# Two pre-norm decoder layers: norms on VectorE, value splits on GpSimd, 16-bit query products and a new order

## The chip, the cores and the metric

One core of a Trainium2 chip. TensorE multiplies, VectorE (DVE), ScalarE (ACT) and GpSimd (POOL) do the rest, SyncE (SP) issues most transfers. The metric is the device time of one execution in microseconds. The kernel before takes 503.5 us (median of three runs, 502.57 to 505.62).

## The reference

16 sequences of 128 tokens with 128 channels go through six residual layers. Each normalises its input first.

```python
def _layernorm(x, axis=-1, eps=1e-05):
    m = jnp.mean(x, axis=axis, keepdims=True)
    v = jnp.var(x, axis=axis, keepdims=True)
    return (x - m) / jnp.sqrt(v + eps)

x = x + _L0_attn_ref(_layernorm(x), ...)             # self0: 16 heads of 8, causal softmax
x = x + _L0_xattn_ref(_layernorm(x), ctx_1024, ...)  # cross0: 8 heads of 64 over 128 context rows
x = x + _L0_ffn_ref(_layernorm(x), ...)              # ffn: ternary weight, inputs rounded to 8 bits
x = x + _L1_attn_ref(_layernorm(x), ...)             # self1: scores clipped to +-10, causal
x = x + _L1_xattn_ref(_layernorm(x), ctx_1024, ...)  # cross1: 16 heads of 64
x = x + _L1_ffn_ref(_layernorm(x), ...)              # moe: softmax gate over 8 experts, gates under 0.1 dropped
```

In the cross layers q = x @ Wq, k = context @ Wk, v = context @ Wv, and the output is softmax(q k / scale) v @ Wo. All values are float32.

## The kernel before

**Stages and order.** Each sequence is one 128x128 tile. The six layers are stages named self0, cross0, ffn, self1, cross1, moe, and each is cut into steps such as `self0.rs` or `cross1.pv.0`. A planner (`all_steps`, `Plan`) knows of each step its engine, a cost, the steps that it needs and the PSUM banks that it takes; the order of the steps on each engine is written out by hand in `ORDER`, as strings of two letters per step, and each engine runs its list in that order with semaphore waits. Several sequences are under way at a time, and an engine that waits for one step holds all that stand behind it in its list. The banks of PSUM (8, single "X" ones for short fills, pairs "S" for scores) are handed out by the plan.

**A norm.** The residual step on VectorE ends with `stats` (line 1010): mean, and variance plus eps. Step `rs` on GpSimd (`rstd`, line 738) raises the variance to -0.5 (line 742), drains, and multiplies the mean by minus that (line 747). Step `nm` on ScalarE (`normalise`, line 887) then makes `xn` as Identity of x with a scale and a bias (line 893). Only sequence 0 of self0 does it on VectorE, with one `tensor_scalar` (line 1221). TensorE turns `xn` over (`xT`, line 1547), ScalarE copies it to `xnT` (`xTe`, helper `take`, line 830).

**A cross layer.** cross0 has one chunk of 8 heads, cross1 two. Step `q` (`four_pairs`, line 1288) multiplies four 128x128 blocks of the query weights with `xnT`, in float32 (line 1291), and ScalarE copies the result (`qe`). Keys and values of the context are made ahead: 6 sequences ahead for cross0, 4 for cross1 (`AHEAD`). Each is a sum of three products of high and low parts (lines 1392 to 1402). For the values, ScalarE writes the high part as bfloat16 into `v_high` (`ve`, line 948), and VectorE subtracts it from PSUM and writes the low part as float16 into `v_low` (`vl`, line 1051).

**The weights of attention.** `s1` makes the scores (line 1333), VectorE their negative maxima (`mx`, line 1045), ScalarE the exponentials e (`ex`, line 865) and their float16 high part (`hi`, line 874). SyncE turns that over by a transposing DMA (`dh`, line 697), GpSimd writes the low part beside it (`lo`, line 781), SyncE turns that over too (`dm`, line 703). `pv` multiplies both with the values, three products per head (lines 1373 to 1375), and VectorE divides by the sums (`nr`, lines 1061 and 1063). The next sequence's `ex` of a chunk waits until `lo` has read e; the next `lo` waits until `dm` has read the low part.

**Other work of GpSimd** that stands around the change: the low parts of the self layers' weights, in place (line 774), the split of their small values (lines 764 and 766), the low parts of large weights once at the start (line 643), the sum over the experts (lines 796 to 802).

Of the kernel before, what the change touches and what calls it, by code (L numbers as in the profile page):

```python
# [28 lines left out]

SHIFT = 7 * math.log(2.0)  # L30
# [53 lines left out]
def all_steps():  # L84
# [9 lines left out]
    def norm(L, source, users, read="xTe"):  # L94
        add(f"{L}.rs", "POOL", 940, [source], [f"{L}.nm"], first=580 if L == "self0" else None,
            last=580 if L == "moe" else None)
        add(f"{L}.nm", "ACT", 380, [but_last(f"{L}.rs") if L == "moe" else f"{L}.rs", source],
            [f"{L}.un" if L == "ffn" else f"{L}.xT"], first=300 if L == "self0" else None, last=170 if L == "moe" else None)
# [3 lines left out]
        made = dict(ffn=["ffn.un"], moe=[but_last("moe.nm"), last_only(source)]).get(L, [f"{L}.nm"])  # L102
        fill(f"{L}.xT", 109, made, f"{L}.{read}", users)
        add(f"{L}.xTe", *(("DVE", 250) if L == "ffn" else ("ACT", 332 if L == "moe" else 166)),
            [f"{L}.xT", *([last_only("moe.nm")] if L == "moe" else [])])

    def self_attention(L, source, maxima, following, loads, loads_out):
# [24 lines left out]
        add(f"{L}.res", "DVE", 835, [f"{L}.y"], [f"{following}.rs"])  # L132

    def keys_values(L, chunks, k_w, v_w):
# [4 lines left out]
        for c in range(chunks):  # L139
            fill(f"{L}.v.{c}", 695, [*context, f"{v_w}.lo"], f"{L}.vl.{c}", [ago(f"{L}.pv.{c}", AHEAD[L])])  # L140
            add(f"{L}.ve.{c}", "ACT", 484, [f"{L}.v.{c}"])
            add(f"{L}.vl.{c}", "DVE", 605, [f"{L}.ve.{c}"])

    def cross_attention(L, source, chunks, following, biased, k_w, v_w, loads):
        keys_values(L, chunks, k_w, v_w)
        norm(L, source, [f"{L}.q.{c}" for c in range(chunks)])
        for c in range(chunks):
            fill(f"{L}.q.{c}", 893, [f"{L}.xTe", loads], f"{L}.qe.{c}", [f"{L}.s1.{c}"])
            add(f"{L}.qe.{c}", "ACT", 487, [f"{L}.q.{c}"])
        for c in range(chunks):  # L150
            add(f"{L}.s1.{c}", "PE", 893, [f"{L}.qe.{c}", second(f"{L}.ke.{c}")], (), "S", f"{L}.ex.{c}")
            add(f"{L}.mx.{c}", "DVE", 1130, [f"{L}.s1.{c}"], [f"{L}.ex.{c}"])
            add(f"{L}.ex.{c}", "ACT", 2060, [f"{L}.mx.{c}"], [f"{L}.lo.{c}"], half=1030)
            add(f"{L}.hi.{c}", "ACT", 940, [f"{L}.ex.{c}"], [f"{L}.dh.{c}"])
            add(f"{L}.dh.{c}", "SP", TURN, [f"{L}.hi.{c}"], [f"{L}.T.{c}"], tail=TURN_TAIL)
            add(f"{L}.lo.{c}", "POOL", 2100, [f"{L}.hi.{c}"], [f"{L}.dm.{c}"])
# [5 lines left out]
        fill(f"{L}.y", 893, [f"{L}.oTe.0"], f"{L}.res", last=1116 if chunks == 2 else None)  # L162
        if chunks == 2:
            add(f"{L}.z", "PE", 893, [f"{L}.y", f"{L}.oTe.1"])
        add(f"{L}.res", "DVE", 840, [f"{L}.{'yz'[chunks - 1]}", *biased], [f"{following}.rs"],
# [304 lines left out]
def decoder(nc, t, out):  # L470
    ctx = ExitStack()
    with ctx:
# [249 lines left out]
        def _(pool):  # L722
# [15 lines left out]
            def rstd(L, i):  # L738
# [876 lines left out]
```

## Time and profile before

| what | value |
|---|---|
| runs | 503.5 us median, 502.57 to 505.62 |
| the profiled execution | 504.29 us, of which the span is 502.5 us |
| granted TensorE clock, mean over the span | 0.983 |
| TensorE busy | 471.4 us, 94% |
| ScalarE busy | 438.6 us, 87% |
| VectorE busy | 404.4 us, 80% |
| GpSimd busy | 383.4 us, 76% |

A line of the page names a group of instructions: source line, engine, operation, tiles, shapes, count, then busy time and mean duration in ns, then the idle time in front of them and what ended it. PE is TensorE, PEld its weight loads, DVE VectorE, ACT ScalarE, POOL GpSimd, SP SyncE. A busy share of the whole span mixes a start, a middle and a tail.

### The profile page before, as it was taken

The page shows a single profiled execution, that of the slowest core. Times are in us where ns is not written, and L with a number is a line of the kernel's source. Part 1 is how long each engine was busy: PE and PEld are TensorE (multiplying, and loading weights), DVE is VectorE, ACT ScalarE, POOL GpSimd, SP SyncE. Part 2 cuts the span into 40 slices and gives each one's busy share as a digit, 9 for nine tenths or more (in the row PEclk, how much of TensorE's full clock was granted, in tenths as well). Part 3 has the DMA queues.
Part 4 walks back from the last instruction along what each step waited for, and adds up shares of the span by engine and source line. Part 5 has one row for each costly group of instructions (what it writes and reads, how often), then busy time and mean ns, then how long its engine had stood idle before and what let it go on. Part 6 is the DMA issues. An engine that isn't in the chain of part 4 may idle for free.

```text
span 502.5 us, 16468 instructions
## 1 busy us (share of the span) xinstructions
PE 471.4 (94%) x5702; PEld 399.1 (79%) x5702; DVE 404.4 (80%) x954; ACT 438.6 (87%) x1180; POOL 383.4 (76%) x465
## 2 busy tenths in 40 slices
PE   7789998999999999999999999999999899999866
PEld 3678786787888898877888888897788788978764
DVE  4598887986888888888889898888987678867645
ACT  4688889999999989998989999999889898999842
POOL 2487587877668878889979888996877599775752
PEclk8799999998999999999999999999999999999989
DMA  6800222205132422531254215243424224233450
GB/s 195 330 3 3 43 43 44 43 10 115 24 68 45 85 44 42 94 65 39 48 92 87 55 29 79 44 90 46 85 53 84 57 44 86 43 65 71 89 97 16
DMA packets 107841, 33.87 MB, mean 67 GB/s; under 512 B 102768, under 2 KB 106224, under 8 KB 107760
## 3 DMA queue, kind: packets, MB, share of 16 engines
q1 hardware_dynamic: 107328, 32.04, 31.8%
q8 instruction: 47, 0.77, 0.6%
q10 hardware_dynamic: 432, 0.79, 0.5%
q14 instruction: 34, 0.28, 0.2%
HBM read 6.50 MB, written 1.05 MB: 15 GB/s over the span
## 4 chain that ended last, share of the span: by engine, by line
PE 59%; ACT 10%; POOL 9%; issue 9%; DMA 3%; POOLq 3%; DVE 3%; SPq 2%; DVEq 1%; ACTq 0%
PE psum L1291 6%; PE psum L1333 5%; PE psum L1419 5%; PE psum L1342 4%; POOL w_self L774 4%; PE psum L1322 4%; POOL e_parts_cross L781 3%; PE psum L1382 3%; ACT w_cross L865 3%; DMA eT_cross<-e_parts_cross 2%; PE psum L1431 2%; PE psum L1392 2%; PE psum L1373 2%; PE psum L1400 2%; PE psum L1355 2%
## 5 line engine op out<-in xcount | busy, mean ns | idle before, releaser
L774 POOL TENSOR_TENSOR w_self<-w_self 128x1024 f16<-128x1024 f32 x64 | 120.9, 1900 | 19.8 <-ACT w_self L854 14.3
L781 POOL TENSOR_TENSOR e_parts_cross<-w_cross,e_parts_cross 128x1024 f16<-128x1024 f32 x48 | 102.6, 2141 | 13.0 <-ACT e_parts_cross L874 13.0
L865 ACT ACTIVATE w_cross<-psum,row_max_cross 128x128 f32<-128x128 f32 x384 | 105.0, 413 | 3.7 <-DVE row_max_cross L1045 3.4
L1045 DVE TENSOR_REDUCE row_max_cross<-psum 128x8 f32<-128x1024 f32 x48 | 58.3, 1219 | 7.9 <-PE psum L1333 7.5
L1333 PE MATMUL psum<-kT_cross,qT_cross 64*128 64x128 f32 x768 | 54.7, 284 | 0.6 <-ACT qT_cross L830 0.6
L1333 PEld LDWEIGHTS psum<-kT_cross,qT_cross 64*128 64x128 f32 x768 | 46.4, 187 | 8.4 <-issue 5.2
L874 ACT ACTIVATE e_parts_cross<-w_cross 128x1024 f16<-128x1024 f32 x48 | 52.6, 1099 | 0.3
L1373 PE MATMUL psum<-v_high_cross,eT_cross 128*128 128x65 bf16 x384 | 40.6, 196 | 5.5 <-DMA eT_cross<-e_parts_cross 3.7
L1373 PEld LDWEIGHTS psum<-v_high_cross,eT_cross 128*128 128x128 f16 x384 | 35.7, 98 | 10.5 <-issue 8.9
L1083 DVE SCALAR_TENSOR_TENSOR w_self<-psum,s_bound 128x1024 f32<-128x1024 f32 x32 | 37.9, 1219 | 4.3 <-PE psum L1322 3.6
L1072 DVE TENSOR_REDUCE row_max_self<-psum 128x8 f32<-128x1024 f32 x32 | 38.9, 1216 | 2.9 <-PE psum L1322 2.8
L1074 DVE TENSOR_TENSOR w_self<-psum,row_max_self 128x1024 f32<-128x1024 f32 x32 | 39.2, 1225 | 2.4
L1374 PE MATMUL psum<-v_low_cross,eT_cross 128*128 128x64 f16 x384 | 40.5, 193 | 0.0
L1375 PE MATMUL psum<-v_high_cross,eT_cross 128*128 128x65 bf16 x384 | 40.4, 194 | 0.0
L1322 PE MATMUL psum<-by_head_self,plain_self 32*128 32x512 f32 x256 | 37.4, 654 | 1.3 <-ACT by_head_self L830 1.1
L848 ACT ACTIVATE w_self<-w_self,shift 128x1024 f32<-128x1024 f32 x32 | 37.1, 1172 | 1.4 <-DVE w_self L1083 1.4
L854 ACT ACTIVATE w_self<-psum 128x1024 f32<-128x1024 f32 x32 | 33.3, 1040 | 5.2 <-PE psum L1342 4.9
L830 ACT ACTIVATE by_head_self<-psum,head_mask 128x128 f32<-128x128 f32 x128 | 37.4, 407 | 0.0
L1051 DVE TENSOR_TENSOR v_low_cross<-psum,v_high_cross 128x512 f16<-128x512 f32 x48 | 32.2, 676 | 6.2 <-ACT v_high_cross L948 5.9
L1063 DVE TENSOR_TENSOR eT_cross<-psum,e_rec_cross 128x512 f32<-128x512 f32 x48 | 33.2, 692 | 3.6
L1374 PEld LDWEIGHTS psum<-v_low_cross,eT_cross 128*128 128x128 f16 x384 | 35.8, 100 | 0.2
L1375 PEld LDWEIGHTS psum<-v_high_cross,eT_cross 128*128 128x128 f16 x384 | 35.9, 97 | 0.0
(221 smaller groups left out, 1539.9 us busy)
## 6 DMA issues: line engine op xcount, KB each, us to landing
eT_cross<-e_parts_cross SPq DMA_TRANSPOSE x96, 3.1
out_dram<-x_all SPq DMA_DIRECT2D x16, 64.0 KB, 2.0
x_all<-in_x SPq DMA_DIRECT2D x1, 768.0 KB, 7.8
cT_all<-in_ctx SPq DMA_DIRECT2D x1, 768.0 KB, 9.6
e_k<-in_e_k SPq DMA_DIRECT2D x1, 512.0 KB, 5.5
e_v<-in_e_v SPq DMA_DIRECT2D x1, 512.0 KB, 6.4
e_q<-in_e_q SPq DMA_DIRECT2D x1, 512.0 KB, 8.6
e_o<-in_e_o SPq DMA_DIRECT2D x1, 512.0 KB, 9.6
```

The lines of the kernel that those rows point to most:

```text
L774: pool.tensor_tensor(L.w_low[u], L.w[u][:], halves(L.w[u][:]), ALU.subtract)\
L781: pool.tensor_tensor(L.e_parts[u][:, UN:2 * UN], L.e[u][:], L.e_parts[u][:, 0:UN], ALU.subtract)\
L865: last = act.activation(L.e[u][:, P * p:P * (p + 1)], S_[:, P * p:P * (p + 1)], ACT.Exp, bias=L.row_max[:, u, p:p + 1])
L874: act.activation(L.e_parts[u][:, 0:UN], L.e[u][:], ACT.Copy).then_inc(L.e_high[u], 1)
L1045: dve.tensor_reduce(L.row_max[:, u, :], group(i, turn)[:].rearrange("p (h k) -> p h k", h=UNIT), AX_X, ALU.max, negate=True).then_inc(L.ma ...
L1072: dve.tensor_reduce(L.row_max[:, u, :], scores, AX_X, ALU.max)
L1074: dve.tensor_tensor(L.diff[u][:].rearrange("p (h k) -> p h k", h=UNIT), scores, L.row_max[:, u, :].unsqueeze(2).broadcast_to([P, UNIT, P]) ...
L1322: last = pe.matmul(group(i, name, u)[:, 512 * half:512 * (half + 1)], L.plain[rows, :], L.by_head[rows, :, :].rearrange("p j n -> p (j n)" ...
L1333: last = pe.matmul(S_[:, at:at + P], L.qT[rows, h // 2, :], kT[rows, h // 2, i % 2, :], start=True, stop=True)
L1373: pe.matmul(out_[:, at:at + XD + 1], e_high, v_high[:, UNIT * c + h, :], start=True, stop=False)
L1374: pe.matmul(out_[:, at:at + XD], e_high, v_low[:, UNIT * c + h, :], start=False, stop=False)
L1375: last = pe.matmul(out_[:, at:at + XD + 1], e_low, v_high[:, UNIT * c + h, :], start=False, stop=True)
```

## The change

Parts of the diff follow, each behind a sentence on it.

The norms of self0, cross0, ffn, self1 and cross1 move from ScalarE to VectorE, as one operation on x, the mean (a scalar per row) and the reciprocal deviation (one column, spread over 128). GpSimd no longer makes the negative mean for them. The norm of moe stays.

```diff
                 power = pool.tensor_tensor(L.rstd[:], L.mean_var[:, 1:2], minus_half[:], ALU.pow)
-                if (L, i) in ((self0, 0), (moe, NSEQ - 1)):
+                if L is not moe or i == NSEQ - 1:
                     power.then_inc(L.rstd_ready, 1)
                     return
                 pool.drain()
...
+            def normalise(L, i):
+                dve.wait_ge(L.rstd_ready, i + 1)
+                if i and L is not ffn:
+                    dve.wait_ge(x_full, full(i - 1, f"{L.name}.xT"))
+                if i and L is ffn:
+                    dve.wait_ge(units_ready, i)
+                dve.scalar_tensor_tensor(out=L.xn[:], in0=x_all[:, i, :], scalar=L.mean_var[:, 0:1],
+                                         in1=L.rstd[:].broadcast_to([P, P]), op0=ALU.subtract, op1=ALU.mult)\
+                    .then_inc(L.xn_ready, 1)
```

The values are written as float32 into one buffer `v`; their high part is the upper half of each word, read as bfloat16, and GpSimd puts the low part as float16 into the lower half. `pv` waits for that (`v_split`).

```diff
-        self.v_high = [self.sb(f"v_high{b}", [P, heads, XD + 1], BF16) for b in range(AHEAD[name])]
-        self.v_low = [self.sb(f"v_low{b}", [P, heads, XD], FP16) for b in range(AHEAD[name])]
+        self.v = [self.sb(f"v{b}", [P, heads, XD + 1]) for b in range(AHEAD[name])]
+        self.v_high = [by_halves(v, BF16)[:, :, :, 1] for v in self.v]
+        self.v_low = [by_halves(v, FP16)[:, :, 0:XD, 0] for v in self.v]
...
+def by_halves(v, dt):
+
+    return v[:].rearrange("p h w -> p (h w)").bitcast(dt).rearrange("p (h w two) -> p h w two", w=XD + 1, two=2)
...
+            def low_values(L, i, u):
+                buffer, heads = i % AHEAD[L.name], slice(UNIT * u, UNIT * (u + 1))
+                pool.wait_ge(*emptied(i, f"{L.name}.v.{u}"))
+                pool.tensor_tensor(L.v_low[buffer][:, heads, :], L.v[buffer][:, heads, 0:XD],
+                                   L.v_high[buffer][:, heads, 0:XD], ALU.subtract).then_inc(L.v_split[u], 1)
```

The low part of the attention weights goes into the first half of the buffer of e itself. So the next exponentials of a chunk wait for the transposition of the low part, and GpSimd waits for nothing there.

```diff
-        self.e_parts = [self.sb(f"e_parts{u}", [P, 2 * UN], FP16) for u in range(self.units)]
+        self.high_plane = [self.sb(f"high_plane{u}", [P, UN], FP16) for u in range(self.units)]
+        self.low_plane = [w[:].bitcast(FP16)[:, 0:UN] for w in self.w]
...
                 pool.wait_ge(L.e_high[u], i + 1)
-                if i:
-                    pool.wait_ge(L.e_turned[u], 16 * i)
-                pool.tensor_tensor(L.e_parts[u][:, UN:2 * UN], L.e[u][:], L.e_parts[u][:, 0:UN], ALU.subtract)\
+                pool.tensor_tensor(L.low_plane[u], L.e[u][:], L.high_plane[u][:], ALU.subtract)\
                     .then_inc(L.e_low[u], 1)
...
                 act.wait_ge(L.max_ready[u], i + 1)
                 if i:
-                    act.wait_ge(L.e_low[u], i)
+                    act.wait_ge(L.e_turned[u], 16 * i)
```

The queries become three float16 products. The weights, times 4096, are split once into high (ScalarE) and low (VectorE). ScalarE writes `xnT` as float16, VectorE its low part from PSUM in a new step `xl`, and `q` waits for that. The copy behind it divides by 4096.

```diff
+            def low_queries(name):
+                dve.wait_ge(hi_ready[name], 1)
+                dve.scalar_tensor_tensor(out=q_low[name], in0=wt[name][:], scalar=Q_UNIT, in1=q_high[name][:],
+                                         op0=ALU.mult, op1=ALU.subtract).then_inc(lo_ready[name], 1)
+
+            def low_x(L, i):
+                name = f"{L.name}.xT"
+                dve.wait_ge(L.xnT_ready, i + 1)
+                dve.tensor_tensor(L.xnT_low[:], bank(i, name)[:, 0:P], L.xnT[:], ALU.subtract)\
+                    .then_inc(emptied(i, name)[0], 1)
...
                 for k in range(4):
-                    col = P * (4 * c + k)
-                    last = pe.matmul(bank(i, name)[:, P * k:P * (k + 1)], w[:, col:col + P], xT,
-                                     start=True, stop=True)
+                    col, out_ = P * (4 * c + k), bank(i, name)[:, P * k:P * (k + 1)]
+                    pe.matmul(out_, w_low[:, col:col + P], L.xnT[:], start=True, stop=False)
+                    pe.matmul(out_, w_high[:, col:col + P], L.xnT_low[:], start=False, stop=False)
+                    last = pe.matmul(out_, w_high[:, col:col + P], L.xnT[:], start=False, stop=True)
                 last.then_inc(x_full, 1)
```

In the planner the steps get new costs and needs, the loads a chain, and the `ORDER` strings of all five engines are new. On GpSimd, `m_w.lo` (2.4 us) moves from before the third pair of self0's low parts to behind the first ones of cross1, and the first value splits stand between the low parts of the start. On SyncE the transposes come in another order.

## Rows read from the trace of the kernel before

**Rows 1.** The page's first part: busy us, share of the span, instructions.
```profile
PE 471.4 (94%) x5702; PEld 399.1 (79%) x5702; DVE 404.4 (80%) x954; ACT 438.6 (87%) x1180; POOL 383.4 (76%) x465
```

**Rows 2.** Busy time by stretch: stretch, length, engines in the header's order, clock, DMA.
```profile
core 0: us, PE busy (x) PEld busy (x) DVE busy (x) ACT busy (x) POOL busy (x), PEclk, DMA share, GB/s
...
20.00:50.00 30.00, 28.42 (x283) 23.93 (x283) 24.33 (x37) 23.47 (x50) 21.34 (x30) 0.97 0.13 51
50.00:150.00 100.00, 94.21 (x1177) 78.94 (x1176) 81.78 (x177) 93.29 (x248) 74.45 (x89) 0.98 0.26 49
150.00:350.00 200.00, 198.08 (x2576) 171.66 (x2576) 174.77 (x412) 188.29 (x525) 171.94 (x206) 1.00 0.34 62
350.00:450.00 100.00, 95.94 (x1175) 82.16 (x1173) 81.31 (x197) 90.93 (x246) 79.52 (x95) 1.00 0.33 62
```

**Rows 3.** The chain that ended last, by engine, from the page.
```profile
PE 59%; ACT 10%; POOL 9%; issue 9%; DMA 3%; POOLq 3%; DVE 3%; SPq 2%; DVEq 1%; ACTq 0%
```

**Rows 4.** VectorE's waits, 150 to 350 us: total, times, longest (first, last).
```profile
DVE row_max_cross L1045 <- PE psum L1333: 2.0, 4, 0.6
...
DVE x_all L1112 <- PE psum L1492: 0.2, 1, 0.2
```

**Rows 5.** The same, 50 to 150 us (first and last).
```profile
DVE a_max L1019 <- ACT xn_ffn L893: 2.5, 2, 1.5
...
DVE e_rec_cross L1061 <- PE psum L1375: 0.2, 1, 0.2
```

**Rows 6.** The chain in order of time, 130 to 136 us: start, us, work.
```profile
130.08 0.03 PE psum L1373
...
131.34 0.12 PE psum L1393
...
133.63 0.89 PE psum L1291 x8
```

**Rows 7.** ScalarE's groups of instructions, 150 to 350 us.
```profile
L830 ACT ACTIVATE qT_cross<-psum 128x512 f32<-128x512 f32 x22 | 13.9, 634 | 0.5 <-PE psum L1291 0.5
L948 ACT ACTIVATE v_high_cross<-psum 128x512 bf16<-128x512 f32 x15 | 9.8, 653 | 0.1
L893 ACT ACTIVATE xn_cross<-x_all,minus_mean_cross,rstd_cross 128x128 f32<-128x128 f32 x14 | 7.3, 523 | 0.8 <-POOL minus_mean_cross L747 0.8
L893 ACT ACTIVATE xn_self<-x_all,minus_mean_self,rstd_self 128x128 f32<-128x128 f32 x14 | 7.3, 519 | 0.0
...
L893 ACT ACTIVATE xn_ffn<-x_all,minus_mean_ffn,rstd_ffn 128x128 f32<-128x128 f32 x7 | 3.6, 509 | 0.0
```

**Rows 8.** VectorE and GpSimd in order of time, 23 to 32 us: start, us, work.
```profile
23.61 3.75 POOL L774 TENSOR_TENSOR w_self<-w_self 128x1024 f16<-128x1024 f32 x2 [3.59 <-ACT w_self L854]
...
25.66 1.78 DVE L1197 TENSOR_SCALAR weighted<-weighted 128x128 f32<-128x128 f32 x1
...
27.32 2.37 POOL L643 TENSOR_TENSOR e_v_lo<-e_v,e_v_hi 128x1024 fp32r<-128x1024 f32 x1
27.52 2.25 DVE L1199 TENSOR_SCALAR ternary<-weighted 128x128 bf16<-128x128 f32 x1
...
31.30 0.29 DVE L1101 TENSOR_TENSOR attn_self<-o_sum_self,psum 128x128 f32<-128x128 f32 x1
...
31.50 0.68 DVE L1051 TENSOR_TENSOR v_low_cross<-psum,v_high_cross 128x512 f16<-128x512 f32 x1
```

**Rows 9.** GpSimd's groups of instructions, 150 to 350 us.
```profile
L774 POOL TENSOR_TENSOR w_self<-w_self 128x1024 f16<-128x1024 f32 x30 | 56.7, 1900 | 2.5 <-ACT w_self L848 1.9 <-ACT w_self L854 0.4
L781 POOL TENSOR_TENSOR e_parts_cross<-w_cross,e_parts_cross 128x1024 f16<-128x1024 f32 x22 | 47.0, 2143 | 5.2 <-ACT e_parts_cross L874 5.2
...
L764 POOL TENSOR_TENSOR v_self<-v_self 128x128 f32<-128x128 f32 x15 | 6.0, 402 | 0.0
```

**Rows 10.** The statistics' line 1013: duration in ns, least, median, most.
```profile
L1013 DVE BATCH_NORM_STATS2 moments_cross<-x_all x32: 294/295/297, 39.5 to 465.2; 128x6 f32<-128x128 f32 x32
```

**Rows 11.** The one norm on VectorE, line 1221: duration likewise.
```profile
L1221 DVE TENSOR_SCALAR xn_self<-x_all,mean_var_self,rstd_self x1: 347/347/347, 5.7 to 5.7; 128x128 f32<-128x128 f32 x1
```

**Rows 12.** DMA issues of the page: times issued, median us to landing.
```profile
eT_cross<-e_parts_cross SPq DMA_TRANSPOSE x96, 3.1
```

More of the change, by code:

```diff
@@ L28 @@
 CLIP = 10.0
+Q_UNIT = 4096.0
 SHIFT = 7 * math.log(2.0)
@@ L94, in norm @@
     def norm(L, source, users, read="xTe"):
[L95 to L98, printed above, removed]
+        if L == "moe":
+            add(f"{L}.rs", "POOL", 940, [source], [f"{L}.nm"], last=580)
+            add(f"{L}.nm", "ACT", 380, [but_last(f"{L}.rs"), source], [f"{L}.xT"], last=170)
+        else:
+            add(f"{L}.rs", "POOL", 580, [source], [f"{L}.nm"])
+            add(f"{L}.nm", "DVE", 200, [f"{L}.rs"], [f"{L}.un" if L == "ffn" else f"{L}.xT"])
         if L == "ffn":
@@ L139, in keys_values, with cross_attention @@
         for c in range(chunks):
[L140 to L144, printed above, removed]
+            fill(f"{L}.v.{c}", 695, [*context, f"{v_w}.lo"], f"{L}.ve.{c}", [ago(f"{L}.pv.{c}", AHEAD[L])])
+            add(f"{L}.ve.{c}", "ACT", 486, [f"{L}.v.{c}"])
+            add(f"{L}.vl.{c}", "POOL", 1000, [f"{L}.ve.{c}"])
+    def cross_attention(L, source, chunks, following, biased, q_w, k_w, v_w):
         keys_values(L, chunks, k_w, v_w)
@@ L161, in cross_attention @@
             add(f"{L}.oTe.{c}", "ACT", 486, [f"{L}.T.{c}"], [f"{L}.{'yz'[c]}"])
-        fill(f"{L}.y", 893, [f"{L}.oTe.0"], f"{L}.res", last=1116 if chunks == 2 else None)
+        fill(f"{L}.y", 893, [f"{L}.oTe.0", "in.more" if L == "cross0" else "in.cross1"], f"{L}.res", last=1116 if chunks == 2 else None)
         if chunks == 2:
             add(f"{L}.z", "PE", 893, [f"{L}.y", f"{L}.oTe.1"])
-        add(f"{L}.res", "DVE", 840, [f"{L}.{'yz'[chunks - 1]}", *biased], [f"{following}.rs"],
+        add(f"{L}.res", "DVE", 840, [f"{L}.{'yz'[chunks - 1]}", *biased], [f"{following}.{'rs' if following == 'moe' else 'nm'}"],
             last=780 if chunks == 2 else None)
-    for name, cost in (("x0", 3535), ("c0", 785), ("b_k", 1080), ("first", 600), ("b_v", 400), ("x1", 600),
-                       ("masks", 1800), ("more", 3600), ("e_k", 1400), ("e_v", 1400), ("x", 2000), ("ctx", 2200), ("self1", 600), ("cross1", 2500), ("moe", 1500)):
-        add(f"in.{name}", "SP", cost, once=True)
+    loads = (("x0", 3600), ("c0", 750), ("b_k", 1150), ("first", 500), ("b_v", 500), ("x1", 500), ("masks", 1500),
+             ("more", 4200), ("e_k", 1450), ("e_v", 1350), ("x", 2000), ("ctx", 2550), ("self1", 800),
+             ("cross1", 2600), ("moe", 1500))
+    for k, (name, cost) in enumerate(loads):
+        add(f"in.{name}", "SP", cost, [f"in.{loads[k - 1][0]}"] if k else [], once=True)
     add("consts", "POOL", 2700, once=True)
@@ L444, in __init__ @@
         self.e_turned = [self.sem(f"e_turned{u}") for u in range(self.units)]
-        self.v_made = [self.sem(f"v_made{u}") for u in range(self.units)]
+        self.v_split = [self.sem(f"v_split{u}") for u in range(self.units)]
 def halves(ap):
@@ L1413, in cross_project @@
                     room(i, y)
+                if i == 0 and c == 0:
+                    load = "more" if L is cross0 else "cross1"
+                    pe.wait_ge(loaded[load], load_count(load))
                 with_x = L is cross1 and i == NSEQ - 1
```

195 lines of the change are left out of this document (102 added, 93 removed).

## The prediction

> **What bounds the kernel now.** I read the busy shares of the page first [rows 1]: TensorE 94%, ScalarE 87%, VectorE 80%, GpSimd 76%. That is a mean over a start, a middle and a tail, so the busy time by stretch comes next [rows 2]. From 150 to 350 us TensorE is busy 198.1 of 200 us at a granted clock of 1.00 (its upper level, 2.4 GHz); ScalarE 188.3, VectorE 174.8 and GpSimd 171.9 stand close behind. The chain that ended last agrees: 59% TensorE, 10% ScalarE, 9% GpSimd, only 3% VectorE [rows 3]. So TensorE sets the pace of the middle, and the reader is to ask of each other engine how much more it can take.
>
> VectorE can take less than its share says. It is idle for 25.2 us of the middle, but its waits for another engine are 16 rows with a sum of 10.3 us, from 2.0 down to 0.2 [rows 4]. The other 14.9 us are short pauses behind its own dependent operations, which stay. So its spare time is 10.3 us of 200. From 50 to 150 us it is 11.4 us in 10 rows [rows 5].
>
> **Queries as 16-bit products.** A chunk of queries now takes 8 TensorE pieces of one chain entry, 0.89 us [rows 6]. After the change it is 12 products of 128 columns. No row has that size; two lie near. A key piece of 256 columns starts 0.12 us after the one before, 0.06 per 128 columns; a values product of 65 columns 0.03 us, 0.06 for 128 [rows 6]. Both carry a weight load of 128 columns each. I take 12 x 0.06 = 0.71 us, 0.18 us less per chunk; 48 chunks give 8.6 us of TensorE. The ends: 0.03 us each, if columns did not count, would save 25 us; 0.12 each would cost 26. Both rows scale with columns, so neither end is likely. VectorE gets 32 low parts of x, 14 of them in the middle (one per normalised x of a cross layer [rows 7]).
>
> **Low parts of the values.** VectorE loses 48 operations, 15 in the middle [rows 7]. One lasts 0.68 us, of which the next operation overlaps some 0.09, as it does with the one in front (31.30 + 0.29 against 31.50 [rows 8]): 0.60 us, 9.0 back in the middle. GpSimd gets them. Its in-place operation takes 0.40 us on 128 elements and 1.90 on 1024 [rows 9], so 1.04 on 512 by a straight line; the ends are half of 1.90 and half of 2.14 with a start of 0.1 on top. That is 15.6 us in the middle against what goes from there (next part). The values in TensorE's products are now every second 16-bit word. The key pieces already stream 4 bytes per column at 0.12 us for 256 columns, the same 0.47 ns per column as the values product [rows 6], so I price the stride at nothing; at half rate it would be 24 x 0.03 = 0.7 us per chunk.
>
> **In-place weights.** ScalarE's next exponentials wait for the transposition of the low part rather than for the subtraction, some microseconds more, once per sequence and chunk. What hides it is the period of a chunk, about 28 us (200 us hold seven FFN norms [rows 7]); GpSimd in turn no longer waits there. Price 0; without that cover, up to 3.1 us [rows 12] for each of 48. The transposes are as many and as large as before; SP's queue only issues them in another order. The split of the two query weights is ScalarE and VectorE work of some 1 us each, once, before the first queries.
>
> **The norms.** GpSimd drops the drain and the negative mean, and ScalarE loses 79 norms of 0.51 us, 40 us of busy time; in the middle 35 (14 + 14 + 7 [rows 7]), 18 us. ScalarE has cover from then on. GpSimd loses about 35 x (0.27 + 0.17) = 15.4 us of operation and pause there, which is what the values bring: no change.
>
> VectorE gets the norms. An operation of 128 elements occupies it for 0.20 us (31.30 to 31.50 [rows 8]): 7.0 us for 35. With 14 low parts of x at the same 0.20 (2.8) and the values gone (9.0), VectorE has 0.8 more in the middle. That would fit ten times over. What decides is whether a norm also waits. The old norm subtracted the mean on ScalarE; the new one reads x and the reciprocal deviation from SBUF as two tensors and writes SBUF, while GpSimd is busy 86% of the middle.
>
> No steady VectorE operation of the kernel before has that form: each has at least one tensor in PSUM, or one input only. The rows bound it. From below: the statistics read x from SBUF and write 6 numbers, and take 294 to 297 ns, whatever GpSimd does [rows 10]: no wait. From above, the nearest shape, 128x128 from SBUF to SBUF: two scalings of the ternary weights took 1.78 and 2.25 us, where the norm of sequence 0, with GpSimd idle, took 0.35 [rows 11]. The first began in GpSimd's pair of operations from 23.61 to 27.36 and ended at 27.44; the second began in the operation from 27.32 to 29.69 and ended at 29.77 [rows 8]. Each waited for the GpSimd operation that was running and went through 0.08 us after it.
>
> I take the upper row, since the norm is nearest to it: same size, nothing in PSUM. The price per norm is then the rest of the running GpSimd operation. For an arrival at any moment that is the sum of n x d x d / 2 over 200 us: 30 x 1.90 x 1.90 = 108 and 22 x 2.14 x 2.14 = 101 [rows 9], some 45 from the short ones: 254 / 400 = 0.63 us. I take 0.6. If each norm met a GpSimd operation at its very start, it would be 171.9 / 206 = 0.83 us [rows 2].
>
> The Trainium skill has a rule for this, in "SBUF — State Buffer", section "Who interferes with whom": a VectorE instruction with two SBUF inputs contends with a GpSimd instruction that reads SBUF, and the one that issues second blocks until the first ends. By that rule each norm waits and the time is the 515 us of the sum below; by the statistics' row it would be 494. The trace agrees for the one-input scalings (1.78 and 2.25 us); no run here shows the two-input form.
>
> **The sum**, against the profiled execution's 504.3 us (span 502.5 and 1.8 around it; 0.8 above the 503.5 median):
> - 150 to 350 us: VectorE gets 0.8 + 35 x 0.6 = 21.8 and has 10.3 free: +11.5. TensorE's saving of 22 chunks is worth nothing there, because VectorE is late: the norm is queued ahead of the maxima and quotients on its in-order engine, ScalarE's exponentials wait for the maxima, and TensorE for the banks that both empty.
> - 50 to 150 us: some 22 norms x 0.6 = 13.2 against 11.4: +1.8.
> - 350 to 450 us: some 16 norms, 9.6, fit in 18.7 idle [rows 2]; TensorE keeps 11 x 0.18: -2.0.
> - The rest, 5 chunks: -0.9.
>
> 504.3 + 11.5 + 1.8 - 2.0 - 0.9 = 514.7. **I forecast 515 us.** With 0.45 per norm it is about 508; with 0.83 the three stretches give +27, 530.
>
> **Rivals.**
> *No wait (faster).* The two-input form behaves as the statistics do. Then VectorE's load stays, TensorE gives 8.6, and ScalarE, busy 93.3 of 100 at 50 to 150 us [rows 2], frees about 2 of the 5.8 us that TensorE idles there: 504.3 - 10.6 = 494 (489 to 498). For it: no row shows the two-input form waiting. Against it: the scalings. It decides below 10 / 35 = 0.28 us per norm.
> *Half hidden.* The new order puts norms where GpSimd pauses or VectorE would wait anyway, 0.3 us each: 35 x 0.3 + 0.8 - 10.3 = +1.0 in the middle, the other 26 chunks give 4.7: 501 (498 to 506). Against it: GpSimd pauses only 28 of 200 us.
> *GpSimd becomes the bound at the start.* From 20 to 50 us it is busy 21.3 of 30 [rows 2]; ten value splits at 1.04 fill that. Without norm waits some 5 us of the 10 gained go: 499. Against it: the values are made several sequences ahead.
>
> **Chances.** Norm waits 0.53 (own range 506 to 524); no wait 0.28; half hidden 0.14; GpSimd 0.05. Range 491 to 524: it leaves out the lower third of "no wait" and the highest waits, under 0.2. About 1%, 5 us, can be told from no change. Faster by over 1% is most of "no wait": 0.27. Within 1%: most of "half hidden" and GpSimd, and the edges: 0.22. Slower by over 1%: 0.51.
>
> **What would show it.** Norm operations on VectorE with a mean near 0.9 us and a maximum near 2.2, each ending just after a GpSimd operation, and VectorE over 90% busy in the middle with TensorE waiting for it: the forecast. Norms at 0.25 to 0.35 us throughout: "no wait". Query groups should stand 0.71 us long in the chain, value splits near 1.04 us on GpSimd, GpSimd's weights at 2.14. The forecast fails if the wait per norm is under 0.28 us, or if the new order leaves VectorE more room than 10 us.

## The result and the profile after

The changed kernel takes 533.1 us (median of 4 runs, 532.1 to 535.0) against 503.8 us of the kernel before in the same session: a ratio of 1.058 (95% interval 1.053 to 1.063). The forecast was 515 us with a range of 491 to 524. The direction was right, and so was the wait of the norms; what that wait costs was not, and the time lies outside the range. Where some executions of a kernel came in a slower state, only the others count here and below.

The page of the changed kernel (its profiled execution took 532.15 us), the busy time by stretch with the columns of [rows 2], and the chain that ended last:

```profile
span 530.1 us, 16680 instructions
...
PE 469.9 (89%) x5894; PEld 393.9 (74%) x5894; DVE 442.9 (84%) x1019; ACT 413.7 (78%) x1103; POOL 414.7 (78%) x434
```

```profile
50.00:150.00 100.00, 88.17 (x1149) 73.41 (x1150) 86.31 (x183) 81.22 (x217) 76.77 (x76) 0.97 0.28 49
150.00:350.00 200.00, 180.60 (x2381) 153.37 (x2378) 178.12 (x405) 160.64 (x438) 162.03 (x170) 0.98 0.33 54
350.00:450.00 100.00, 93.62 (x1210) 79.08 (x1209) 87.83 (x211) 83.25 (x225) 84.85 (x86) 1.00 0.40 67
```

```profile
PE 41%; DVE 23%; DVEq 11%; issue 10%; ACT 6%; POOL 5%; DMA 2%; POOLq 0%; SPq 0%; ACTq 0%
```

VectorE's busy time grew by 38.5 us over [rows 1], and TensorE and ScalarE work less of each of these stretches than in [rows 2]. In the chain VectorE stands at 23% plus 11% of its sequencer, where [rows 3] has 3% and 1%. Where the time went can be read from TensorE's instructions: a pass now has 5894 instead of 5702. At the old pace 150 to 350 us would hold 2576 x 5894 / 5702 = 2663 of them; it holds 2381, so this stretch fell behind by 200 x (1 - 2381 / 2663) = 21 us. From 50 to 150 us it is 5.6 us, from 350 to 450 us 0.4. Together that is 27.2 of the 27.6 us by which the span grew. (This takes instructions as a measure of work, so it is an estimate.)

The norms of the changed kernel, with the least, median and longest duration in ns, and who waited for them:

```profile
L1054 DVE SCALAR_TENSOR_TENSOR xn_self<-x_all,mean_var_self,rstd_self x32: 310/392/2521, 6.0 to 467.5; 128x128 f32<-128x128 f32 x32
L1054 DVE SCALAR_TENSOR_TENSOR xn_cross<-x_all,mean_var_cross,rstd_cross x32: 336/352/2204, 34.1 to 494.0; 128x128 f32<-128x128 f32 x32
L1054 DVE SCALAR_TENSOR_TENSOR xn_ffn<-x_all,mean_var_ffn,rstd_ffn x16: 343/1385/2369, 70.9 to 457.0; 128x128 f32<-128x128 f32 x16
...
who waited for it (us, times):
  PE psum L1596: 13.2, 11
```

The shortest are like the single norm of [rows 11], the longest as long as a GpSimd operation. In order of time, GpSimd and VectorE around one of them (start, us, work):

```profile
132.79 2.39 POOL L666 TENSOR_TENSOR m_w_lo<-m_w,m_w_hi 128x1024 fp32r<-128x1024 f32 x1
135.14 1.10 POOL L808 TENSOR_TENSOR v_cross<-v_cross 128x512 f16<-128x512 f32 x1
```

```profile
132.36 0.69 DVE L1107 TENSOR_TENSOR eT_cross<-psum,e_rec_cross 128x512 f32<-128x512 f32 x1
132.96 2.37 DVE L1054 SCALAR_TENSOR_TENSOR xn_ffn<-x_all,mean_var_ffn,rstd_ffn 128x128 f32<-128x128 f32 x1
135.37 0.29 DVE L1060 TENSOR_REDUCE a_max<-xn_ffn 128x1 f32<-128x128 f32 x1
```

The norm began 0.17 us after a GpSimd operation and ended 0.15 us after that had ended (132.79 + 2.39 = 135.18). The timeline shows the norms in 78 rows: 34 are under 0.45 us (mean 0.346), and of the 44 longer ones 39 end 0.12 to 0.16 us behind the end of a GpSimd operation. By the groups of the page the norms take 24.2 + 22.4 + 20.6 = 67.2 us; at 0.345 each they would take 27.6. So the waits are 39.6 us, 0.50 per norm; in the stretch from 150 to 350 us they are 18.0 us in 33 rows, 0.54 each. From 50 to 150 us they are 10.5 us, from 350 to 450 us 6.0.

### The profile page after: what moved, and what is told of

Same layout as the page of the kernel before. It is cut to its first block, busy times and chain, and to the rows that moved or that the text cites. A ratio compares the mean times of both kernels' runs of the same rounds, so it can differ in the third digit from the quotient of the medians.

```text
span 530.1 us, 16680 instructions
## 1 busy us (share of the span) xinstructions
PE 469.9 (89%) x5894; PEld 393.9 (74%) x5894; DVE 442.9 (84%) x1019; ACT 413.7 (78%) x1103; POOL 414.7 (78%) x434
## 4 chain that ended last, share of the span: by engine, by line
PE 41%; DVE 23%; DVEq 11%; issue 10%; ACT 6%; POOL 5%; DMA 2%; POOLq 0%; SPq 0%; ACTq 0%
PE psum L1380 5%; PE psum L1469 4%; DVE row_max_cross L1097 4%; DVEq L1164 3%; DVEq L1117 3%; POOL w_self L797 3%; PE psum L1429 3%; PE psum L1389 2%; PE psum L1369 2%; DVE w_self L1118 2%; DVE xn_ffn L1054 2%; DVEq L1142 2%; DVE xn_cross L1054 2%; DVE w_self L1127 2%; ACT w_cross L894 2%
## 5 line engine op out<-in xcount | busy, mean ns | idle before, releaser
L797 POOL TENSOR_TENSOR w_self<-w_self 128x1024 f16<-128x1024 f32 x64 | 122.5, 1922 | 20.2 <-ACT w_self L877 11.9
L802 POOL TENSOR_TENSOR w_cross<-w_cross,high_plane_cross 128x1024 f16<-128x1024 f32 x48 | 103.1, 2151 | 24.6 <-ACT high_plane_cross L903 24.2
L894 ACT ACTIVATE w_cross<-psum,row_max_cross 128x128 f32<-128x128 f32 x384 | 103.9, 397 | 13.3 <-DVE row_max_cross L1097 13.2
L903 ACT ACTIVATE high_plane_cross<-w_cross 128x1024 f16<-128x1024 f32 x48 | 51.4, 1079 | 0.4
L808 POOL TENSOR_TENSOR v_cross<-v_cross 128x512 f16<-128x512 f32 x48 | 50.2, 1057 | 0.0
L1420 PE MATMUL psum<-v_cross,eT_cross 128*128 128x65 bf16 x384 | 43.0, 197 | 6.6 <-DVE w_self L1127 3.1
L1420 PEld LDWEIGHTS psum<-v_cross,eT_cross 128*128 128x128 f16 x384 | 37.5, 99 | 10.2 <-issue 9.4
L1421 PE MATMUL psum<-v_cross,eT_cross 128*128 128x64 f16 x384 | 42.9, 195 | 0.0
L1422 PE MATMUL psum<-v_cross,eT_cross 128*128 128x65 bf16 x384 | 42.9, 196 | 0.0
L1421 PEld LDWEIGHTS psum<-v_cross,eT_cross 128*128 128x128 f16 x384 | 37.6, 99 | 0.3
L1389 PE MATMUL psum<-ident,w_self 128*128 128x128 f32 x256 | 34.1, 276 | 4.1 <-DVE w_self L1118 4.0
L1422 PEld LDWEIGHTS psum<-v_cross,eT_cross 128*128 128x128 f16 x384 | 37.3, 98 | 0.0
```

The source lines that it names most:

```text
L797: pool.tensor_tensor(L.w_low[u], L.w[u][:], halves(L.w[u][:]), ALU.subtract)\
L802: pool.tensor_tensor(L.low_plane[u], L.e[u][:], L.high_plane[u][:], ALU.subtract)\
L808: pool.tensor_tensor(L.v_low[buffer][:, heads, :], L.v[buffer][:, heads, 0:XD], L.v_high[buffer][:, heads, 0:XD], ALU.subtract).then_inc(L ...
L894: last = act.activation(L.e[u][:, P * p:P * (p + 1)], S_[:, P * p:P * (p + 1)], ACT.Exp, bias=L.row_max[:, u, p:p + 1])
L903: act.activation(L.high_plane[u][:], L.e[u][:], ACT.Copy).then_inc(L.e_high[u], 1)
L1420: pe.matmul(out_[:, at:at + XD + 1], e_high, v_high[:, UNIT * c + h, :], start=True, stop=False)
```

## The experiments

All are medians, and each ratio is to runs of the kernel before on the same chip, with its 95% interval. Where a step changes its engine, the kernel's order had to be made anew; it was searched with the planner's own costs until the planned end was near that of the kernels above. The last run of the first group says what one such order was worth.

### Do the waits cost the time?

**Norms that read one tensor.** The order and all other parts of the change stay.

```diff
-                dve.scalar_tensor_tensor(out=L.xn[:], in0=x_all[:, i, :], scalar=L.mean_var[:, 0:1],
-                                         in1=L.rstd[:].broadcast_to([P, P]), op0=ALU.subtract, op1=ALU.mult)\
+                dve.tensor_scalar(L.xn[:], x_all[:, i, :], L.mean_var[:, 0:1], L.rstd[:], ALU.subtract, ALU.mult,
+                                  accum_out=L.unused[:]).then_inc(L.xn_ready, 1)
```

> The changed kernel, its order kept; each of the 80 norms reads x alone as a tensor and takes mean and reciprocal deviation as two scalars per partition, and writes a sum that nobody reads (which keeps it a slow one-input form). Theory 'wait': the norms' 67 us fall to about 80 x (0.35 + 0.14 for the read-out of the sum) = 39 us, no norm lasts over 0.6 us, VectorE's busy time falls by some 28 us and the time by nearly as much: 505 us (498 to 512). Theory 'order and values': the new order, or GpSimd's value splits, are what costs; then the time stays at 525 us or more although the norms are short.

Measured: 500.2 us, ratio 0.994 (0.991 to 0.997). In this form the second operation serves the sum, so the multiplication by the reciprocal deviation is missing from `xn`, here and in the four kernels below that build on it. The norms of it, least, median and most:

```profile
L1055 DVE TENSOR_SCALAR_CACHE_REDUCE xn_self<-x_all,mean_var_self,rstd_self x32: 374/399/407, 5.8 to 438.5; 128x128 f32<-128x128 f32 x32
L1055 DVE DVE_READ_ACCUMULATOR xn_self<-x_all,mean_var_self,rstd_self x32: 78/83/86, 6.1 to 438.9; 128x1 f32 x32
```

None of the 80 waits (the longest of the others took 407 ns as well). The page of this run:

```profile
PE 465.1 (93%) x5894; PEld 389.7 (78%) x5894; DVE 409.0 (82%) x1099; ACT 411.8 (82%) x1103; POOL 411.8 (82%) x434
```

VectorE's busy time fell from 442.9 to 409.0 us (the 39.6 us of waits, less what this longer form adds), and 32.9 us of time went with 33.9 us of VectorE. All of the loss, and a little more, hangs on the waits.

**The plain one-tensor form.**

```diff
-                dve.scalar_tensor_tensor(out=L.xn[:], in0=x_all[:, i, :], scalar=L.mean_var[:, 0:1],
-                                         in1=L.rstd[:].broadcast_to([P, P]), op0=ALU.subtract, op1=ALU.mult)\
+                dve.tensor_scalar(L.xn[:], x_all[:, i, :], L.mean_var[:, 0:1], L.rstd[:], ALU.subtract, ALU.mult)\
```

> The changed kernel in its own order; each norm is the plain form with one tensor from SBUF and two scalars per partition, no sum written out. Theory 'SBUF to SBUF': it waits for GpSimd as the scalings of the ternary weights did (1.78 and 2.25 us), mean 0.65 to 0.85 us: 527 to 535 us. Theory 'second tensor': only the second tensor input waits, so norms are at 0.25 to 0.4 us throughout and the time is that of the form with the sum, or less: 495 to 501 us.

Measured: 538.2 us, ratio 1.071 (1.064 to 1.078). The norms of the ffn layer, least, median and most:

```profile
L1054 DVE TENSOR_SCALAR xn_ffn<-x_all,mean_var_ffn,rstd_ffn x16: 338/1423/2317, 69.6 to 461.0; 128x128 f32<-128x128 f32 x16
```

It waits as the two scalings of [rows 8] did. So it isn't the second tensor alone: the plain one-tensor form from SBUF to SBUF waits too. The Trainium skill says in "SBUF — State Buffer", section "Who interferes with whom", that two SBUF inputs contend with GpSimd's reads and that `tensor_scalar` can, and it excepts the form that also writes out its accumulator. The three measured means (0.84 us with two tensors, 0.92 plain, 0.40 with the sum) agree with it.

**The norms alone**, added to the kernel before: of the diff shown ahead, `normalise` on VectorE and the two lines of `rstd`.

> The kernel before with the norms alone on VectorE, in the two-input form; values and queries as before, order searched again to the same planned end. Theory 'wait': VectorE keeps its 48 value splits and gets norms of 0.35 us plus about 0.5 us of wait each, some 67 us on top of 404; with some 87 us that it can not fill this gives 545 to 560 us, worse than the whole change. Theory 'order and values': norms of 0.35 us, about 504 us.

Measured: 533.1 us, ratio 1.060 (1.055 to 1.066). The group of its cross norms in the page's form (busy us, mean ns):

```profile
L1024 DVE SCALAR_TENSOR_TENSOR xn_cross<-x_all,mean_var_cross,rstd_cross 128x128 f32<-128x128 f32 x32 | 25.9, 808 | 2.0 <-POOL rstd_cross L743 1.8
```

The norms alone cost as much as the whole change. They take 25.9 + 20.7 + 12.1 = 58.7 us, so their waits are 31 us and not 40; GpSimd, which has no value splits here, is busy 365.5 us and not 414.7. VectorE, which keeps those, is busy 451.8 us. The 545 to 560 us that I had expected charged the 67 us of the changed kernel's norms in full.

**The norms back on ScalarE**, the rest of the change kept.

```diff
-            add(f"{L}.rs", "POOL", 580, [source], [f"{L}.nm"])
-            add(f"{L}.nm", "DVE", 200, [f"{L}.rs"], [f"{L}.un" if L == "ffn" else f"{L}.xT"])
+            add(f"{L}.rs", "POOL", 940, [source], [f"{L}.nm"])
+            add(f"{L}.nm", "ACT", 380, [f"{L}.rs", source], [f"{L}.un" if L == "ffn" else f"{L}.xT"])
```

> The changed kernel with the 80 norms back on ScalarE (GpSimd makes the negative mean again), the order searched again with the kernel's own costs to nearly the same planned end. Theory 'wait': VectorE loses 67 us, ScalarE gets back 40, and the queries' saving of TensorE time shows at last: 499 us (493 to 507). Theory 'order and values': what is left of the change still costs, over 515 us.

Measured: 504.8 us, ratio 1.004 (1.001 to 1.007). The loss is gone, but the gain that I expected (499 us) isn't there: the chain now reads

```profile
PE 30%; POOL 28%; POOLq 12%; ACT 11%; issue 9%; DMA 4%; DVE 3%; SPq 2%; DVEq 1%; ACTq 0%
```

with GpSimd busy 431.2 us. With ScalarE's norms GpSimd has to make the negative mean again, beside the value splits.

**Another order for the change**, and **another order for the kernel before**, both searched.

> All parts of the change, but its order made from the order of the kernel before by moving only the steps that change engine, and then searched with the kernel's own costs. Theory 'wait': the norms wait in any order that does not know of GpSimd: 533 us (524 to 542), norms with a mean of 0.75 to 0.9 us. Theory 'order': the order of the change is what costs; this one gives below 520 us.

Measured: 535.2 us, ratio 1.064 (1.058 to 1.069); the norms take 68.8 us. The order of the change was not the cause.

> The kernel before with nothing changed but its order: scrambled and then searched with the kernel's own costs, as the orders of the other experiments were, to the same planned end. It tells how much such a new order is worth by itself: 504 us (500 to 508) if the searched orders can be compared; if it comes out slower by more than that, that much of the single-part results is their order.

Measured: 506.4 us, ratio 1.006 (1.003 to 1.009). This searched order costs some 2.7 us; it is only one, and the results with a searched order are to be read with that much doubt.

### Why was VectorE's idle time no cushion?

To the form without waits I added useless maxima on VectorE (0.28 us each, 0.18 of busy time behind one another), in three ways.

```diff
+                for _ in range(2):
+                    dve.tensor_reduce(extra[:, len(spent):len(spent) + 1], x_all[:, i, :], AX_X, ALU.max)
+                    spent.append(i)
```

> The form without waits (the sum written out, 500.2 us) with one useless maximum over x, 128x128 from SBUF, behind each of the 80 norms: some 0.21 us of VectorE each, always the same and with no wait for GpSimd, 17 us in all; the norms themselves are not later. Theory 'VectorE's time counts, whatever spends it' (the waits cost 30.7 us of time for 33.9 us of VectorE): 515 us (511 to 519). Theory 'idle time takes it up', as the prediction had it (10.3 + 11.4 + 18.7 us free): 500 to 505 us.

Measured: 508.7 us, ratio 1.013 (1.008 to 1.018).

```profile
PE 469.2 (93%) x5894; PEld 390.6 (77%) x5894; DVE 423.6 (84%) x1179; ACT 413.1 (82%) x1103; POOL 412.0 (81%) x434
```

> The same with two such maxima behind each norm, some 34 us of VectorE, as much as the waits of the changed kernel took. Theory 'VectorE's time counts': 530 us (524 to 536), the time of the changed kernel. Theory 'it is the unevenness of the waits (0 to 2 us) that costs': even pieces are taken up better, 505 to 515 us.

Measured: 519.6 us, ratio 1.035 (1.030 to 1.039).

```profile
PE 471.3 (91%) x5894; PEld 392.8 (76%) x5894; DVE 438.4 (85%) x1259; ACT 414.0 (80%) x1103; POOL 412.2 (80%) x434
```

The first 14.6 us cost 8.5, the next 14.8 cost 10.8. By the intervals of the ratios the first step is worth between 5 and 14 us, so there is no sign of a free part at the start. Neither theory's number is met: by the medians, a quarter to two fifths of even work is taken up.

With the same lines ahead of the norm:

> The form without waits, with the two useless maxima ahead of each of the 80 norms and not behind it: the same 29 us of VectorE as in the run with two behind (519.6 us), but now each norm and the products behind it are 0.4 us later too, as they are with a wait. Theory 'the lateness of the norm itself is the rest of the price': 528 us (525 to 533). Rival 'the unevenness of the waits, or GpSimd held up in its turn, is the rest': no later than with the two behind, 517 to 522 us.

Measured: 522.5 us, ratio 1.038 (1.035 to 1.041). That the norm itself is late costs 2.9 us by the medians; the intervals of the two ratios overlap, so it may be nothing.

```diff
-                for _ in range(2):
+                for _ in range(8 if len(norms) % 4 == 0 else 0):
```

> The form without waits, with the same 160 useless maxima ahead of the norms as in the run with two ahead of each (522.5 us), but eight of them, 1.7 us, ahead of every fourth norm and none ahead of the others: spread about as the waits are. Theory 'unevenness is the rest of the price': 530 us (526 to 536), the changed kernel's time. Rival 'what GpSimd loses in its turn is the rest': 519 to 524 us, as with the even pieces.

Measured: 525.9 us, ratio 1.044 (1.037 to 1.051). Large pieces cost 3.4 us more than even ones, again with overlapping intervals. So of the 32.9 us of the waits, 19.4 are shown as the price of 29.4 us of even VectorE work; lateness and unevenness come to 6.3 by the medians of runs on different chips, and only their sum stands out of the noise, and barely. The remaining 7.2 has two parts that were only argued: VectorE's difference is 33.9 and not 29.4 us, which at 10.8 / 14.8 is 3.3, and for the last 4 us there is no experiment. Two things may be among it. One is GpSimd's own loss: with the waits its busy time is 414.7 us, without them 411.8, and its longest split of cross weights takes 2288 ns, without them 2152 (the changed kernel first, then the form without waits):

```profile
L802 POOL TENSOR_TENSOR w_cross<-w_cross,high_plane_cross x48: 2123/2142/2288, 53.4 to 508.3; 128x1024 f16<-128x1024 f32 x48
```

```profile
L803 POOL TENSOR_TENSOR w_cross<-w_cross,high_plane_cross x48: 2123/2140/2152, 51.9 to 476.8; 128x1024 f16<-128x1024 f32 x48
```

The other is TensorE's clock. On average over its runs it is 0.974 in the changed kernel, 0.982 with the uneven pieces, 0.985 with the even ones and 0.989 in the form without waits. The lowest stretch of the middle, behind 5 us in which TensorE was busy for only 3.5, stands at 0.66, so partly at the lower of its two levels, 1.2 GHz:

```profile
300.00:310.00 10.00, 8.93 (x115) 7.87 (x117) 7.67 (x16) 5.43 (x13) 6.88 (x7) 0.66 0.46 54
```

The form without waits is at 1.00 from 50 to 450 us. No run here separates the clock from the waits that go with it.

### Where did the queries' saving go?

**Queries alone** (with the in-place weights, which make room in SBUF for the parts of the query weights), and **value splits alone**, each added to the kernel before.

> The kernel before with the queries as three 16-bit products, and with the in-place weights that make room in SBUF for the query weights' parts; norms on ScalarE and values on VectorE as before, order searched again with the kernel's own costs. A group of queries takes 0.67 us in the changed kernel's trace against 0.89. Theory 'TensorE sets the pace of the middle': 48 x 0.22 = 10.6 us of TensorE go and VectorE (+9 us in pauses) hides the 32 low parts of x: 495 us (490 to 499). Theory 'three engines close together': ScalarE (188 of 200 us) takes over and about a third is left: 500 us (498 to 504).

Measured: 503.7 us, ratio 1.002 (0.998 to 1.005). Of the 10.6 us nothing came through; if the order is charged with its 2.7 us, about a sixth, and by the interval at most about a third.

> The kernel before with the value splits alone on GpSimd, in place; norms on ScalarE, queries as before, order searched again. GpSimd goes from 383 to some 433 us, VectorE from 404 to 375. Theory 'GpSimd becomes the bound': its middle would need 172 + 15.6 of 200 us with no slack for the waits on it; 508 us (505 to 514). Theory 'hidden': the values are made several sequences ahead, so the time stays at 504 us (501 to 505).

Measured: 504.7 us, ratio 1.004 (1.001 to 1.007). Nothing was lost either; VectorE's 27 us less, with GpSimd at 430.1 us, gave nothing.

**TensorE's time taken away** in the kernel before, with its own order.

```diff
-                    last = pe.matmul(bank(i, name)[:, P * k:P * (k + 1)], w[:, col:col + P], xT,
+                    last = pe.matmul(bank(i, name)[:, P * k:P * (k + 1)], halves(w[:, col:col + P]), halves(xT),
```

> The kernel before in its own order, with one 16-bit product of the upper halves in place of each full-precision query product: the low parts of x and of the query weights are left out, nothing is added anywhere. A group of queries should fall from 0.89 to 0.22 us, 32 us of TensorE in all. Theory 'TensorE sets the pace' (the prediction's reading of 198.1 busy us of 200): 475 us (470 to 482). Theory 'no single engine does': the other engines stand at 172 to 188 of 200 and the chain runs through all of them, so a small part comes through: 496 us (490 to 502).

Measured: 502.5 us, ratio 0.994 (0.990 to 0.998). A group of queries stands in the chain with 0.25 us now where it stood with 0.89 (8 pieces [rows 6]):

```profile
149.70 0.25 PE psum L1291 x4
```

That is some 31 us for 48 groups, and some 3 of it came through, by the ratio. The single runs spread from 495.8 to 503.1 us. Their mean granted clock is 0.983, against 0.991 of the kernel before beside them, and the two at 0.990 and 0.993 took 5 and 8 us less than its 503.9. So a part of the saving may have gone into the clock, but no run gave more than 8 of the 31 us. Its stretch from 150 to 350 us (the profiled execution took 505.5 us):

```profile
150.00:350.00 200.00, 189.52 (x2471) 158.48 (x2472) 174.16 (x412) 189.21 (x524) 172.50 (x205) 1.00 0.35 62
```

TensorE is idle for 10.5 us now instead of 1.9, ScalarE, VectorE and GpSimd stand where [rows 2] has them, and the time is nearly the same. TensorE alone did not set the pace.

**ScalarE's and GpSimd's time taken away on top.**

```diff
-                act.activation(L.e_parts[u][:, 0:UN], L.e[u][:], ACT.Copy).then_inc(L.e_high[u], 1)
+                act.activation(L.e_parts[u][:, 0:UN // 2], L.e[u][:, 0:UN // 2], ACT.Copy).then_inc(L.e_high[u], 1)
```

> The kernel before with single 16-bit query products (502.7 us, 32 us of TensorE away) and with ScalarE copying only the upper half of the columns of the cross weights' high part: 48 x 0.5 = 25 us of ScalarE away too. Left out: low parts of the queries, and half of the high parts (ones or zeros stand there). Theory 'TensorE and ScalarE set the pace together': 480 us (474 to 488). Theory 'all four engines are in turn': 492 to 500 us.

Measured: 497.1 us, ratio 0.987 (0.980 to 0.993). ScalarE is busy 420.2 us, where it was 438.6.

```diff
-                pool.tensor_tensor(L.e_parts[u][:, UN:2 * UN], L.e[u][:], L.e_parts[u][:, 0:UN], ALU.subtract)\
+                pool.tensor_tensor(L.e_parts[u][:, UN:3 * UN // 2], L.e[u][:, 0:UN // 2], L.e_parts[u][:, 0:UN // 2], ALU.subtract)\
```

> The same, and GpSimd makes only half of the columns of the cross weights' low part: some 48 x 1.0 = 50 us of GpSimd away as well. Theory 'TensorE and ScalarE together': the same time as without this, within 3 us. Theory 'all four engines are in turn': another 8 to 15 us less than without this.

Measured: 495.8 us, ratio 0.985 (0.979 to 0.990). What these two kernels leave out of the cross weights' parts stays zeros or ones.

```profile
PE 447.8 (91%) x5510; PEld 367.3 (74%) x5510; DVE 402.6 (82%) x954; ACT 419.9 (85%) x1180; POOL 339.0 (69%) x468
```

With some 31 us of products less for TensorE, 19 us less for ScalarE and 44 us less for GpSimd (339.0 busy instead of 383.4), the time moved by 1.5% in all, and the intervals of neighbouring steps overlap. What is left untouched is VectorE, as the stretch from 150 to 350 us shows:

```profile
150.00:350.00 200.00, 190.97 (x2489) 158.74 (x2489) 175.93 (x410) 182.54 (x531) 151.95 (x210) 1.00 0.38 61
```

That would fit VectorE as the engine with the least room, but ScalarE is still busy for 182.5 of 200 us, and the kernel with the value splits alone took 27 us from VectorE for no gain while GpSimd rose. Which engines would have to shrink together for the time to fall stays open.

### Is there a version that beats both?

GpSimd could make the norm itself behind its reciprocal deviation, with the 16-bit queries, or the second tensor could lie in PSUM. First GpSimd:

```diff
+                pool.tensor_scalar(L.xn[:], x_all[:, i, :], L.mean_var[:, 0:1], L.rstd[:], ALU.subtract, ALU.mult)\
+                    .then_inc(L.xn_ready, 1)
```

> Queries as three 16-bit products, value splits left on VectorE, and the 80 norms on GpSimd itself, right behind the reciprocal deviation, in place of its negative mean: ScalarE loses its 40 us of norms, VectorE gets none, GpSimd some 10 to 15 us more. Theory 'balance': no engine but TensorE is over 85% busy, and the queries' 10.6 us come through: 492 us (487 to 498). Rival 'GpSimd's queue': the norms stand behind splits of 1.9 to 2.1 us on an in-order engine and come late, so nothing is gained: 500 to 508 us.

Measured: 508.4 us, ratio 1.011 (1.003 to 1.018). The group of its cross norms (busy us, mean ns):

```profile
L771 POOL TENSOR_SCALAR xn_cross<-x_all,mean_var_cross,rstd_cross 128x128 f32<-128x128 f32 x32 | 25.5, 797 | 2.4
```

The negative mean, which it replaces, takes 260 ns: 80 x 0.54 = 43 us. GpSimd rose from 383.4 to 426.5 us, not by 10 to 15.

Then PSUM:

```diff
-            fill(f"{L}.y", 223, [f"{L}.oTe", loads_out], f"{L}.res")
+            fill(f"{L}.y", 223, [f"{L}.oTe", loads_out], f"{following}.nm")
...
+                deviation = bank(i, source)[:, 256:257]
+                dve.tensor_copy(deviation, L.rstd[:])
+                dve.drain()
                 dve.scalar_tensor_tensor(out=L.xn[:], in0=x_all[:, i, :], scalar=L.mean_var[:, 0:1],
-                                         in1=L.rstd[:].broadcast_to([P, P]), op0=ALU.subtract, op1=ALU.mult)\
+                                         in1=deviation.broadcast_to([P, P]), op0=ALU.subtract, op1=ALU.mult)\
```

> All of the change, but with the norms' second tensor in PSUM: for four layers VectorE copies the reciprocal deviation (128x1) into the bank of the layer's last products, which is held until the norm, and multiplies from there; the 16 norms of the first layer are on ScalarE. Order searched again. Theory 'the second tensor from SBUF is what waits': norms at 0.35 to 0.45 us without exception, 502 us (497 to 508). Rival 'two tensors wait wherever they lie': 525 us or more.

Measured: 503.7 us, ratio 1.000 (0.996 to 1.004).

> The version with the norms' second tensor in PSUM (503.7 us), its order searched longer. If the searched order is what keeps it from the 500.2 us of the form with the sum: 501 us (498 to 504). If the copies and the longer hold of the banks do: 503 to 505 us again.

Measured: 501.2 us, ratio 0.995 (0.992 to 0.997), the best kernel here that does the whole work. Its norms and copies:

```profile
L1064 DVE SCALAR_TENSOR_TENSOR xn_cross<-x_all,mean_var_cross,psum x32: 346/347/349, 34.3 to 464.6; 128x128 f32<-128x128 f32 x32
...
L1062 DVE COPY psum<-rstd_cross x32: 149/152/163, 34.0 to 464.4; 128x1 f32<-128x1 f32 x32
```

Two tensors, one of them in PSUM: not one of 64 norms waits (346 to 349 ns in all three groups). Against the changed kernel that is 32 us; against the kernel before it is half a percent, about what an order is worth.

## Why the prediction was right and wrong

**The price of a norm's wait held.** Forecast 0.6 us each, measured 0.50 over all and 0.54 in the middle, most ending just behind GpSimd operations. Choosing the two scalings [rows 8] over the statistics [rows 10] was right. The statistics' row stays true (one input, six numbers out: no wait), but it did not tell of a 128x128 output. The kernel before does have three VectorE operations with two SBUF inputs, once at the start; GpSimd was idle beside them, so they could not decide it. One of them:

```profile
7.37 0.69 DVE L643 TENSOR_TENSOR cT_all_lo<-cT_all,cT_hi 128x512 fp32r<-128x512 f32 x1
```

**VectorE's idle time as a cushion: this step failed.** The sum subtracted 10.3 us of waits for other engines [rows 4] from the 21.8 us that came in, and 11.4 and 18.7 in the stretches beside it. VectorE's waits in the middle, after (13 rows, sum 8.5; first and last):

```profile
DVE e_rec_cross L1105 <- PE psum L1422: 2.2, 2, 1.9
...
DVE x_all L1162 <- issue: 0.2, 1, 0.2
```

So of 10.3 us only 1.8 were taken up. The 10.3 were too many to begin with: four of the 16 rows are "issue", in which VectorE waited for nothing that the profile shows, and not for another engine.

```profile
DVE attn_self L1101 <- issue: 0.6, 2, 0.3
...
DVE psum L1099 <- issue: 0.4, 1, 0.4
...
DVE psum L1142 <- issue: 0.4, 1, 0.4
DVE g_rec L1145 <- issue: 0.4, 1, 0.4
```

Without such rows the waits for other engines went from 8.5 to 7.0 us. As I read it, an engine waits for others at certain moments, and a delay at other moments does not fall there: it makes the others late, and VectorE waits for them afterwards as before. The middle lost 21 us and not 11.5; 50 to 150 us, with 10.5 us of norm waits, lost 5.6 and not 1.8; 350 to 450 us, with 6.0, lost 0.4 where I had a gain of 2.0. In these two stretches the cushion did take up a part: VectorE's waits, all rows, went from 11.4 to 7.8 us and from 11.2 to 5.1 (the same clock times hold other work in the two kernels, so this is rough). The longest rows from 350 to 450 us, before and after:

```profile
DVE e_rec_cross L1061 <- PE psum L1375: 3.1, 3, 2.2
```

```profile
DVE row_max_cross L1097 <- PE psum L1380: 1.2, 3, 0.8
```

The runs with useless maxima show the price without GpSimd: the very first 14.6 us cost 8.5.

**TensorE sets the pace: this step failed too.** 198.1 busy us of 200 and 59% of the chain [rows 2, 3] were taken as proof. With some 31 us of its products gone the time moved by 0.6%, and by 1.6% at most in a single run. Busy time counts a product until its modelled end, and a chain through an engine that is always queued shows that engine. So the rival "no wait" at 494 us was mis-sized as well: the form without waits gives 500.2, above that rival's 489 to 498.

**Prices of single operations held.** Products of the queries start 0.056 us apart in the form without waits (232 pairs from 150 to 350 us), 12 x 0.056 = 0.67 us per group against the forecast's 0.71; the changed kernel has 0.05 to 0.07 for 198 of its pairs there and 0.10 to 0.11 for the other 23. Value splits on GpSimd take 1046 ns in the median (forecast 1.04). The products with the strided values start 0.0324 us apart against 0.0307 before (506 and 530 pairs), 0.04 us per chunk where I had nothing. GpSimd's weights stay at 2142 ns. ScalarE's later exponentials were not tested by themselves; the kernel with the queries alone has them too and lost nothing.

**The rivals.** "Half hidden" and "GpSimd at the start" are out: the waits came to 0.50 us and not 0.3, and GpSimd's value splits alone cost 0.4%, no more than a new order. The upper end of the range was too low because it left the cushion in: without it the sum is 504.3 + 21.8 + 13.2 + 9.6 = 549 us, and the time lies between that and the forecast, as the runs with useless work would have it. It left out even the 530 us that the prediction gave for 0.83 us per norm.

## What to carry to other kernels

Before an operation moves to VectorE, ask of its form whether it reads two tensors from SBUF or is a plain `tensor_scalar` from SBUF to SBUF (both waited here), and what GpSimd does at that time; a second tensor in PSUM took the waits away here without losing any of the work. Do not subtract an engine's idle time from work that is added at other moments: charge it at the 0.6 to 1.0 that these runs show until a run with useless work of the same size says otherwise. And test "this engine sets the pace" by taking its time away in the unchanged order before a saving on it is counted.

## What the hardware showed beyond that

GpSimd's `tensor_scalar` on 128x128 with two scalars took 797 ns, twice its subtraction of two 128x128 tensors in place (402 ns [rows 9]). The VectorE form that writes out its sum took 0.40 us and 0.08 for the read-out, between the 0.35 of a norm that meets nothing and the 0.84 of the mean norm. And GpSimd seems to be held up by such norms in its turn: its busy time is 414.7 us in the changed kernel and 414.1 in the other order, against 411.8 to 412.3 in the five kernels with the sum written out.
